# Rows of the last two batches routed through a scratch and tile table of their own, with their tail of attention set between expert tiles

## What is computed

```python
x = L0_attn_x
x = _layernorm(x + attention(x), axis=-1)
# the experts
gate_probs = softmax(xf @ gate_w.T)
topk_scores, topk_idx = top_k(gate_probs, 2)
topk_scores = topk_scores / sum(topk_scores)
h = relu(einsum('td,ehd->teh', xf, w1) + b1)
expert_out = einsum('teh,edh->ted', h, w2) + b2
out = einsum('ted,te->td', expert_out, combine)
x = _layernorm(x + out, axis=-1)
```

## Time and profile before

| | us |
|---|---|
| median of 3 runs | 1186.22 (1182.94 to 1187.09) |
| profiled execution | 1182.22 |
| its span, first to last instruction | 1180.3 |
| PE, PEld, DVE, ACT, POOL busy | 1044.4, 512.6, 971.2, 901.0, 588.4 |
| mean granted TensorE clock | 0.972 of full |

### The profile page before, as it was taken

How to read it: one execution, slowest core, us unless ns; L and a number is a source line. 1 busy time by engine, 2 the same in 40 slices (tenths; PEclk the granted TensorE clock), 3 DMA queues, 4 the chain that set the end, 5 groups by cost and what they waited for, 6 DMA issues and landing times. The chain is left out here.

```text
span 1180.3 us, 24741 instructions
## 1 busy us (share of the span) xinstructions
PE 1044.4 (88%) x7711; PEld 512.6 (43%) x7711; DVE 971.2 (82%) x2117; ACT 901.0 (76%) x1161; POOL 588.4 (50%) x823
## 2 busy tenths in 40 slices
PE   4589999999999999999999999897459999999967
PEld 2232223232232222222323222222249999999952
DVE  4688898989989999899899998991458888888845
ACT  1177888788788887887878878778259999999827
POOL 1124318256273472643825627314347777777745
PEclk9899999999999999999999999999669999999989
DMA  2832242232322413324234232200022222222246
GB/s 72 262 100 74 63 118 72 84 106 71 109 70 82 136 47 107 91 64 130 74 83 115 65 98 71 79 14 19 21 72 70 67 71 68 70 69 69 64 181 255
DMA packets 105461, 104.88 MB, mean 89 GB/s; under 512 B 21608, under 2 KB 82834, under 8 KB 105376
## 3 DMA queue, kind: packets, MB, share of 16 engines
q1 hardware_dynamic: 94912, 81.88, 24.6%
q0 software_dynamic: 8448, 16.93, 4.5%
q10 hardware_dynamic: 2016, 4.98, 1.1%
HBM read 56.06 MB, written 47.39 MB: 88 GB/s over the span
## 5 line engine op out<-in xcount | busy, mean ns | idle before, releaser
L802 DVE TENSOR_REDUCE row_max<-score_ps 128x2 f32<-128x1024 f32 x512 | 618.4, 1220 | 71.8 <-PE score_ps L573 68.7
L688 ACT ACTIVATE probs<-score_ps 128x1024 f32<-128x1024 f32 x512 | 522.0, 1023 | 115.6 <-PE score_ps L555 93.6
L849 POOL DMA_INDIRECT routed_d<-rows,slot_i x128 | 126.7, 990 | 316.6 <-DVE slot_i L771 270.2
L536 PE MATMUL av_ps<-probs,v_one 128*9 128x512 f32 x2048 | 267.7, 595 | 6.8 <-ACT probs L688 5.9
L573 PE MATMUL score_ps<-k_stack,q_stack 48*128 48x512 bf16 x1024 | 199.6, 387 | 49.9 <-ACT probs L688 26.3
L555 PE MATMUL score_ps<-q_stack,k_stack 51*128 51x512 bf16 x1024 | 199.1, 386 | 18.3 <-DVE row_max L802 13.7
L1110 ACT ACTIVATE w_cur<-experts 128x1156 f32 x136 | 158.5, 1167 | 36.6 <-PEq L415 17.2
L555 PEld LDWEIGHTS score_ps<-q_stack,k_stack 51*128 51x128 bf16 x1024 | 48.9, 92 | 298.4 <-issue 166.2
L1206 POOL DMA_INDIRECT y_d<-y_out,place x136 | 137.0, 1007 | 44.5 <-issue 44.5
L1067 PE MATMUL up_ps<-xt_sb,w_cur 128*128 128x128 f32 x1088 | 146.2, 278 | 0.5 <-DVE xt_sb L1143 0.4
L1075 PE MATMUL down_ps<-w_cur,hidden_r 128*128 128x128 f32 x1088 | 143.4, 275 | 0.0
(11 more groups left out here) (186 smaller groups left out, 1110.6 us busy)
## 6 DMA issues: line engine op xcount, KB each, us to landing
k_stack<-k_stack_d SPq DMA_DIRECT2D x128, 96.0 KB, 2.5
q_stack<-q_stack_d SPq DMA_DIRECT2D x128, 96.0 KB, 2.5
x_rows_sb<-routed_d SPq DMA_DIRECT2D x136, 65.0 KB
q_stack_d<-q_parts SPq DMA_DIRECT2D x32, 192.0 KB
k_stack_d<-k_parts SPq DMA_DIRECT2D x30, 192.0 KB
x_in<-L_attn_x SPq DMA_DIRECT2D x16, 256.0 KB, 3.7
q_stack_d<-q_parts SPq DMA_DIRECT2D x32, 128.0 KB
x_res<-L_attn_x SPq DMA_DIRECT2D x16, 256.0 KB, 3.5
```

What stands on the lines that cost most here:

```text
L536: last = nc.tensor.matmul(av_ps[32 * g:32 * g + V_COLS, :], v_one[n.parity][:, kb, HG * hg + g, :], probs[:, (2 * j + g // 2) % P_RING, g ...
L688: nc.scalar.activation(probs[:, s % P_RING, :, :], exp_bank(b, s)[:, :, :], ACT.Exp).then_inc(S["exp_done"], 1)
L802: nc.vector.tensor_reduce(row_max[:, m // (STEPS // 2), :, m % (STEPS // 2)], max_bank(b, s)[:, :, :], AX.X, ALU.max).then_inc(S["red_done ...
L849: nc.gpsimd.indirect_dma_start(routed_d, bass.IndirectOffsetOnAxis(ap=slot_i[n.parity][:, w, t:t + 1], axis=0), rows[n.parity][:, w, t, :] ...
```

## The change

- The batches 0 to 13 scatter to `routed_a`, batches 14 and 15 (`LATE = 2`) to `routed_b`, each with its own row counts and padding. There are two tile tables, one after the other in `tile_expert` and `tile_row`: `TILES_A` = 119 and `TILES_B` = 23, together 142 tiles.
- `schedule` stops after the body of batch 15. Behind it stand only the last product with the values, the last `y_out`, the residual of batch 15 and the places of batch 14. Table A is computed on DVE in the steps 14 to 28 of the body of batch 15. POOL's last four scatters of batch 13 wait for the score steps 22, 24, 26 and 28. SP stores A's padding, waits for the scatters up to batch 13 and for table A, and issues the loads of the first eight tiles, all before the attention block ends.
- What is left of batches 14 and 15 stands as `attention(j)` in each engine's expert loop, tile j giving the place; 88 tiles are written out (`UNROLL`), the loop takes 6 passes of 8, and 6 tiles follow. Table B is computed on DVE at tiles 28 to 41; the scatters stand on POOL at every fourth tile from 12 to 72.
- `misc_ps` lives on into the tile block, which has one `xt_ps` instead of two; PE waits for `xt_out` of a tile before it transposes the next.
- SP's tile loads are written out. Before load 64 it stores B's padding, before load 119 it waits for table B, all padding and all scatters.

```diff
-TILES = 2 * B * T // P + E
+TILES_A = 2 * (B - LATE) * T // P + E - 1
+TILES_B = 2 * LATE * T // P + E - 1
+TILES = TILES_A + TILES_B
...
-                for n in range(-2, B + 2):
+                for n in range(-2, B):
...
+                            if b.c == B - 1 and 14 <= s <= 14 + TABLE_STEPS:
+                                tile_table(dve, table_a, s - 14, 0, TILES_A, CAP, row_base[:, :])
...
                         if prev2 and cur and not proj:
-                            scatter(p2, 4, 8)
+                            for k in range(4, 8):
+                                pool.wait_ge(S["st_done"], b.count(STEPS, 14 + 2 * k))
+                                scatter(pool, p2, k, k + 1)
...
                     schedule(pool, body)
+                    residual(pool, Batch(0, B - 1))
+                    places(pool, Batch(0, B - 2))
...
+                    sp.wait_ge(table_a, 1)
+                    store_pads(sp, routed_a, CAP, (B - LATE) * T)
+                    sp.wait_ge(pads_stored, 32 + 16 * E)
                     for n in range(2):
-                        sp.wait_ge(scattered[n], B // 2 * 8 * 16)
+                        sp.wait_ge(scattered[n], (B // 2 - 1) * 8 * 16)
+                    sp.wait_ge(table_a, TABLE_STEPS)
+                    for t in range(RING):
+                        load_tile(sp, t, None)
...
-                for u in range(RING):
-                    step(0, u)
-                with engine.Fori(1, TILES // RING - 1) as i:
+                for t in range(UNROLL):
+                    step(*divmod(t, RING))
+                with engine.Fori(UNROLL // RING, TILES // RING) as i:
                     for u in range(RING):
                         step(i, u)
...
+                    for t in range(RING, TILES):
+                        if t == 64:
+                            sp.wait_ge(table_b, 1)
+                            store_pads(sp, routed_b, CAP_B, LATE * T)
+                        if t == TILES_A:
+                            sp.wait_ge(table_b, TABLE_STEPS)
+                            sp.wait_ge(pads_stored, 32 + 2 * 16 * E)
+                            for n in range(2):
+                                sp.wait_ge(scattered[n], B // 2 * 8 * 16)
+                        load_tile(sp, t, M["half_done"])
...
                 @block.tensor
+                        if j == 0:
+                            pe.wait_ge(S["yn_sb"], n15.count(HG, 3))
+                            y_transpose(pe, n15, 3)
+                        elif j == 2:
+                            pe.wait_ge(S["yn_sb"], n15.count(HG, 4))
+                            y_to_rows(pe, n15)
+                        elif j == 4:
+                            pe.wait_ge(S["ynt_sb"], n15.count(1, 1))
+                            project_out(pe, n15)
+                        elif j == 7:
+                            pe.wait_ge(S["res_ready"], n15.count(1, 1))
+                            pe.wait_ge(S["top_step"], n14.count(TOP_STEPS, 13))
+                            rank(pe, n14)
+                        elif j == 13:
+                            pe.wait_ge(S["slot_step"], n14.count(SLOT_STEPS, 2))
+                            pe.wait_ge(S["x1_ready"], n15.count(QT, QT))
+                            x1_to_rows(pe, n15)
+                        elif j == 15:
+                            pe.wait_ge(S["x1t_sb"], n15.count(1, 1))
+                            gate(pe, n15)
+                        elif j == 24:
+                            pe.wait_ge(S["logits_sb"], n15.count(1, 1))
+                            pe.wait_ge(S["top_step"], n15.count(TOP_STEPS, 13))
+                            rank(pe, n15)
...
+                        attention(tile_index(i, u))
                         if has_next:
+                            pe.wait_ge(M["xt_out"], i * RING + (u + 1))
                             x_transpose(ni, nu)
                         up(i, u)
...
                 @block.scalar
+                        if j == 2:
+                            second_out(act, n14)
+                            y_rows_out(act, n15)
+                        elif 8 <= j <= 11:
+                            scale_out(act, n15, j - 8)
+                        elif j == 13:
+                            x1_rows_out(act, n15)
+                        elif j == 15:
+                            logits_out(act, n15)
+                        elif j == 20:
+                            second_out(act, n15)
...
                 @block.vector
+                        if j == 0:
+                            y_normalise(dve, n15, 3)
+                            for k in (6, 7):
+                                choose(dve, n14, k)
...
+                        elif j == 4:
+                            layernorm(dve, n15)
+                        elif j == 5:
+                            dve.wait_ge(S["stats_ready"], n15.count(QT, QT))
+                            moments(dve, n15)
...
+                        elif 16 <= j <= 23:
+                            for k in (2 * j - 32, 2 * j - 31):
+                                choose(dve, n15, k)
...
+                        elif 28 <= j < 28 + TABLE_STEPS:
+                            tile_table(dve, table_b, j - 28, TILES_A, TILES_B, CAP_B, base_b[0:1, :])
...
                 @block.gpsimd
+                        if j == 6:
+                            deviation(pool, n15)
+                        elif 12 <= j < 44 and j % 4 == 0:
+                            if j == 12:
+                                rows_ready(pool, n14)
+                            scatter(pool, n14, j // 4 - 3, j // 4 - 2)
+                        elif j == 14:
+                            places(pool, n15)
+                        elif 44 <= j < 76 and j % 4 == 0:
+                            if j == 44:
+                                rows_ready(pool, n15)
+                            scatter(pool, n15, j // 4 - 11, j // 4 - 10)
```

670 lines of the change are left out of this document (387 added, 283 removed).

## The result

The changed kernel is **slower**, by 1.1%: 1195.91 us median (four runs, 1195.90 to 1197.04) against 1184.58 for the kernel before in the same comparison, ratio 1.0112 (95% interval 1.0094 to 1.0129; below, each run has its ratio to the kernel before and this interval). The profiled execution took 1195.9 with a span of 1193.4; before it was 1182.22 and 1180.3. The forecast was 1172.3. Of all executions told of here one, of run 13, was in a slow state of the core (1253.1 us), and no ratio counts it.

A forecast was written before the change was run, and what follows sets the result against it. It took the tiles as bound by PE, with one hole before them. Hole -31.9, six tiles +11.4, PE's pieces +3.6 and stalls +5.0 gave -11.9, forecast 1172.3 us; 8 in 10 from 1164 to 1182.

The forecast's parts named there:

- The hole, -31.9: Between attention and expert tiles: first expert matmul at 839.2 instead of 871.1, gain 31.9 us, bounds 28.9 to 35.6.
- The cold start stays: First three tiles: the lower clock at their beginning remains, 6.3 us; about 2 us gained if the clock stays up.
- Six tiles +11.4: Tile stage: 142 tiles against 136, at 1.903 us each, add 11.4 us.
- PE's pieces +3.6: Tile stage: PE's own y_to_rows, project_out, x1_to_rows, gate and two ranks add 3.6 us.
- DVE and ACT stalls +4.0: Tile stage: stalls from the tail's pieces, 3.0 us on DVE and 1.0 us on ACT.
- Single `xt_ps`, 0: Tile stage: one transposed-row buffer instead of two costs nothing at the steady pace, with 0.6 us of cover.
- POOL, +1.0, bad end +8.7: Tile stage, steps 12 to 72: sixteen routed scatters of 1.27 us on POOL cost 1.0 us, at the bad end 8.7.
- SP's pad stores, 0: Before load 64: eight pad stores, 8.8 us, cost nothing while POOL is less than 0.6 us late, else 1 to 2.
- The end, 0: After the last y scatter: the end unchanged at 45 us.
- The rule weighed: DVE/GpSimd port lock: 0.3 us per meeting, 5 us more in range only; by the skill's figure 40 us and slower.
- POOL takes over as the bound: Rival, steps 12 to 76: POOL's bad end, +7.7, 1180 us, or 1185 with 0.3 more per scatter; chance 0.17.
- The slower case: Rival, tile stage: lower clock stays, each cold tile costs 1.9 us more, 1193; or a large port lock; chance 0.04.

The follow-up runs named there:

- run 13: Deeper pipeline of run 9 with relu, bias and down each a tile later still, all 142 tiles written out without the loop: 1192.85 us, ratio 1.0068.
- run 1: Changed kernel without its 16 routed scatters in the tile stage, last 23 tiles loading pad rows: 1172.31 us, ratio 0.9894.
- Run 3: Changed kernel with two buffers for the transposed rows from tile 28 on (misc_ps as second), no wait for xt_out there: 1197.31 us, ratio 1.0101.
- run 2: Changed kernel with three 128x128 multiplications on POOL in place of each routed scatter, otherwise as run 1: 1171.59 us, ratio 0.9891.
- run 6: Changed kernel without pacing in batch 14's body, transpose and xt_out two tiles ahead from tile 28: 1189.88 us, ratio 1.0054.
- run 9: As run 6, but two tiles ahead from the first tile, and y_bias, y_out and the y scatter one tile later: 1191.48 us, ratio 1.0069.

## Why the prediction was wrong, step by step

The sum was off by 25.0 us: 16.9 in the stage, 5.1 at the end, 3.0 in the hole.

- **What bounds the kernel.** Right that only the hole lay open, that PE bounds the tiles and that work added on PE is paid in full (run 1). But the stalls were priced by how full each engine is, and most of the loss came in by late signals, with no engine at its limit.
- **The hole, -31.9; measured -28.9,** the end of the bounds. SP's loads began at 831.22 and not 828.1, since the attention ended 3.3 later. The prediction took batch 15's time as unchanged. The pacing waits act in batch 14's body too, and POOL's splitting of batch 15's maxima, which stands behind them, began at 780.73 in place of 777.72. Without pacing there the attention's last copy stands at 831.7 to 834.8 in eight profiles, with it at 835.1 to 838.7 in four, and in the six of the kernel before's form at 831.9 to 835.7: so the pacing costs some 2.8 on the mean, and the rows of before were of an execution at the early end. SP's loads were not quite the last wait either: by the engines' records SP left the block at 839.47 and POOL, whose leaving had been put at nothing, at 839.70, 9.2 us after its last operation. In all thirteen runs of this form `up(0)` comes 2.4 us after the later of the two. Fewer loads on SP alone would have won 0.2 us.
- **The cold start stays:** right, 6.35 us for the first stretch (6.30 in the earlier trace rows), though at a mean clock of 0.68 and not 0.60.
- **Six tiles +11.4, PE's pieces +3.6, DVE and ACT stalls +4.0.** Run 1 tells these apart from the scatters: 278.8, so 278.8 - 261.2 - 15.0 = 2.6 of stalls. The places were right too: layernorm (PE waits 0.69 at 855.80), and x1_to_rows (1.50 at 871.67).
- **Single `xt_ps`, 0:** right. Run 3 gave a second one back and won nothing.
- **POOL, +1.0, bad end +8.7: this is the step that failed.** It measured 19.3. "A routed scatter is 0.96 + 0.31 = 1.27" priced it as time on POOL. That time was right (0.97 each) and run 2 shows that it is indeed nearly free (stage 280.1 against 278.8). What was missing is that among the tiles a scatter close to its neighbours makes PE's signals late, by up to 2.1 us, so that DVE, and then PE, waits. Closeness is just what the prediction counted on when it let POOL "go round in 1.61" to catch up. Its own sign misled too: "a period above 1.95 us a tile in steps 30 to 76 says POOL". The period was 2.25, and POOL was idle for a quarter of the time.
- **It could have been read before.** The prediction used to show that POOL catches up, and didn't look at what DVE did in such a stretch. The kernel before has one at 1097 to 1110, seven scatters 1.61 to 1.62 apart:

```profile
1100.66 1.01 POOL L1206 DMA_INDIRECT y_d<-y_out,place  x1 [0.16 <-issue]
...
1102.12 0.29 DVE L1148 TENSOR_TENSOR y_bias<-down_ps,w_cur 128x128 f32<-128x128 f32 x1 [0.97 <-PE down_ps L1075]
1102.28 1.01 POOL L1206 DMA_INDIRECT y_d<-y_out,place  x1 [0.17 <-issue]
...
1108.53 0.29 DVE L1148 TENSOR_TENSOR y_bias<-down_ps,w_cur 128x128 f32<-128x128 f32 x1 [0.84 <-PE down_ps L1075]
...
1109.58 0.82 PE L1067 MATMUL up_ps<-xt_sb,w_cur 128*128 128x128 f32 x5 [0.45 <-DVE xt_sb L1143]
```

  DVE waits 0.97 and 0.84 for a down, where the usual wait ahead of `y_bias`, 103 of them in that stage, is 0.3 at most, and PE has one of its few waits of the stage. Laid beside a clean tile, that is the mechanism at half its size.
- **SP's pad stores, 0:** right for the changed kernel only because PE was late anyway. Once it is not, PE waits for the load behind them: 5.1 us in run 6, 2.2 in run 9.
- **The end, 0; measured +5.1.** The steps after the last tile are the same. POOL stayed in the last block for 9.1 us after its last operation, 2.5 before, where the span ended 1.7 us after POOL had left; now it ends 0.2 after.
- **The rule weighed.** The prediction set aside the port lock of the Trainium skill ("SBUF — State Buffer", "SBUF: two separate sides") since the rows showed 0.3 us. For the scatter's own length that holds: the sixteen took 962 to 972 ns. (Its rows had one long scatter too few: a second, at 858.42, took 1.31, and it too began during an operation of DVE on two inputs.) The rule's outcome (slower) came about, by another way; run 2's arithmetic on POOL, which also reads SBUF, costs nothing.
- **The rivals.** "POOL takes over as the bound" had the place right and the mechanism wrong: POOL is busy for 73% there. The slower case was put on the lower clock and on the port lock; the clock was 1.00 from 848 us on, and no scatter got longer. No rival held a late signal.

## What to carry to other kernels

Before adding a DMA that POOL issues to a loop, look at how far apart its neighbours are and how many steps ahead the bounding engine's input is made; price it by what the other engines wait for in the closest such spot of the old trace, not by its length. If it can't be a plain transfer of another queue, give the bounding engine a lead of two steps in everything that it waits for (run 9 gave with one hand and took with the other) and spread the scatters: the same work then cost nothing. Idle time on an engine says only that its instructions fit, not that their side effects do.
